# Mixer: the out projection takes y and W_out as single fp32 operands instead of hi and lo halves

## The reference, cut to what matters

```
zxbcdt = x @ W_in                               # 256 -> 512 + 768 + 8
xBC = silu(causal_conv(xBC, 4 taps) + conv_b)   # -> xs, B, C
h = h * exp(dt*A) + dt * x * B ; y = h . C      # scan over tokens, 8 heads of 64, state 128
y = (y + D_skip * xs) * silu(z)
y = y * rsqrt(mean(y*y) + 1e-5) * rms_w
out = y @ W_out                                 # 512 -> 256   <- the product that is changed
y1 = out + x ; g = y1 @ glu_w + glu_b
y2 = y1 + a * sigmoid(gate) ; layer norm ; gate ; add to x
```

## Time and profile before

| | us |
|---|---|
| median of 3 runs | 2222.96 (2219.68, 2222.96, 2231.39) |
| the profiled execution | 2228.17 |
| its span, first to last instruction | 2226.4 |
| PE busy | 1658.3 (74%) |
| DVE busy | 1479.1 (66%) |
| ACT busy | 1053.1 (47%) |
| POOL busy | 1005.1 (45%) |

### The profile page before, as it was taken

One profiled execution on the slowest core, in us unless ns is written; L12 is line 12 of the kernel. 1 busy time (PEld: TensorE's weight loads), 2 busy tenths in 40 slices (PEclk: granted clock), 3 DMA queues, 4 the chain that ended last, 5 costly groups with the idle time before them and its releaser, 6 DMA issues. The chain is left out here.

```text
span 2226.4 us, 37571 instructions
## 1 busy us (share of the span) xinstructions
PE 1658.3 (74%) x10724; PEld 1424.5 (64%) x10725; DVE 1479.1 (66%) x3407; ACT 1053.1 (47%) x2135; POOL 1005.1 (45%) x905
## 2 busy tenths in 40 slices
PE   4757989988999889989887456565319999999300
PEld 4745777777777777777776455454319999999300
DVE  4635788878887788788876566666424444444488
ACT  1315556555655665565564334343206666665200
POOL 1202434443444444334443377777735666666300
PEclk7558999999999999999999666666659999999755
DMA  5421101110111011011010345454334555555599
GB/s 175 153 80 45 35 25 39 39 34 25 39 34 38 26 39 34 24 39 34 29 30 15 115 147 173 145 168 153 131 122 149 177 174 172 176 173 167 211 402 361
DMA packets 148926, 242.12 MB, mean 109 GB/s; under 512 B 24960, under 2 KB 95616, under 8 KB 148608
## 3 DMA queue, kind: packets, MB, share of 16 engines
q1 hardware_dynamic: 122752, 169.77, 24.1%
q0 software_dynamic: 26112, 71.62, 8.8%
HBM read 132.75 MB, written 108.56 MB: 108 GB/s over the span
## 5 line engine op out<-in xcount | busy, mean ns | idle before, releaser
L1997 POOL DMA_INDIRECT ys_dram<-byo,bx x272 | 261.3, 961 | 171.6 <-ACT byo L1930 94.6
L985 DVE SCALAR_TENSOR_TENSOR cv<-xc,convw,cv 128x256 f32<-128x256 f32 x576 | 294.3, 575 | 20.8 <-ACT cv L856 20.8
L1652 POOL DMA_INDIRECT xs_dram<-rows,dest x256 | 264.2, 1032 | 91.9 <-issue 77.1
L1173 POOL TENSOR_TENSOR state<-state,par 128x512 f32<-128x512 f32 x64 | 126.0, 1968 | 283.0 <-PE bank L746 283.0
L1966 DVE TENSOR_TENSOR bff<-bgs,bank 128x256 f32<-128x256 f32 x136 | 57.3, 421 | 212.8 <-ACT bgs L1914 212.8
L1930 ACT ACTIVATE byo<-bank,bx 128x256 f32<-128x256 f32 x272 | 114.3, 472 | 145.3 <-DMA ys_dram<-byo,bx 145.0
L104 PE MATMUL bank<-wh,bhh 128*128 x544 | 160.7, 295 | 8.1 <-ACT bhh L1907 6.0
L106 PE MATMUL bank<-wh,bhl 128*128 x544 | 154.3, 284 | 0.0
L105 PE MATMUL bank<-wl,bhh 128*128 x544 | 153.8, 283 | 0.0
L1184 POOL TENSOR_TENSOR y1l<-y,y1h 128x512 fp32r<-128x512 f32 x32 | 76.2, 2382 | 155.3 <-ACT y1h L912 155.3
L721 PE MATMUL bank<-masked,after 128*128 128x512 f32 x256 | 124.6, 610 | 21.4 <-ACT dec L886 21.4
(11 more groups left out here) (257 smaller groups left out, 5514.0 us busy)
## 6 DMA issues: line engine op xcount, KB each, us to landing
bx<-xs_dram SPq DMA_DIRECT2D x272, 129.0 KB
cy<-ys_dram SPq DMA_DIRECT2D x64, 512.0 KB, 9.2
px<-in_x SPq DMA_DIRECT2D x16, 512.0 KB, 3.6
h_t<-phT SPq DMA_DIRECT2D x16, 512.0 KB, 4.1
hN<-h_t SPq DMA_DIRECT2D x32, 256.0 KB, 2.7
hT<-h_t SPq DMA_DIRECT2D x32, 256.0 KB, 2.6
xr<-in_x SPq DMA_DIRECT2D x32, 256.0 KB, 2.6
x_dram<-xr SPq DMA_DIRECT2D x32, 256.0 KB, 2.0
```

Source lines behind the costliest of these rows:

```text
L985: dve.scalar_tensor_tensor(cv[b][:, m, :], xc[b][:, m, tap:tap + GROUP], convw[:, m, tap:tap + 1], cv[b][:, m, :], ALU.mult, ALU.add).then ...
L1173: pool.tensor_tensor(s, s, par[b][:, 3, c, :].unsqueeze(2).to_broadcast([P, H, HD]), ALU.mult).then_inc(sdec_done[b], 1)
L1652: pool.indirect_dma_start(out=xs_dram[:, :], out_offset=bass.IndirectOffsetOnAxis(ap=dest[n % 2][:, c, k:k + 1], axis=0), in_=rows[n % 2][ ...
L1997: pool.indirect_dma_start(out=ys_dram[:, :], out_offset=bass.IndirectOffsetOnAxis(ap=x[s][:, n, D:D + 1].bitcast(U32), axis=0), in_=yo[s % ...
```

## The change

W_out is kept as one fp32 tile (in place of wout_hi and wout_lo), yT as one fp32 tile (in place of yTh and yTl). ACT still copies both (its outputs are now plain fp32). DVE's subtraction for the W_out piece and its two `split_yT` a half are gone, with their semaphores; whoever waited for yTl waits for yT. `project_out` issues 8 fp32 matmuls of 256 columns in place of 24 fp32r ones. All other pieces keep their order.

```diff
-        pieces.append((t["W_out"], wout[0][:, :, :].rearrange("p a b -> p (a b)"),
-                       wout[1][:, :, :].rearrange("p a b -> p (a b)")))
+        pieces.append((t["W_out"], wout[:, :, :].rearrange("p a b -> p (a b)"), None))
...
+                    if pieces[n][2] is None:
+                        return
                     dve.wait_ge(hi_done, n + 1)
                     dve.tensor_tensor(pieces[n][2], raw[n][:, :], pieces[n][1].bitcast(F32), ALU.subtract)
...
-        wout = [sb(f"wout_{h}", [P, KI, D], F32R) for h in ("hi", "lo")]
+        wout = sb("wout", [P, KI, D])
...
-        yTh = both("yTh", [P, KI, GROUP], F32R)
-        yTl = both("yTl", [P, KI, GROUP], F32R)
+        yT = both("yT", [P, KI, GROUP])
...
                 def project_out(b, i):
-                    pe.wait_ge(yTh_done[b], CH * i + CH)
-                    pe.wait_ge(yTl_done[b], CH * i + CH)
+                    pe.wait_ge(yT_done[b], CH * i + CH)
                     pe.wait_ge(y1s_done[b], CH * i + CH)
                     for m in range(KD):
                         for k in range(KI):
-                            last = split3(pe, Q(b, 2)[:, m * GROUP:(m + 1) * GROUP],
-                                          wout[0][:, k, m * P:(m + 1) * P], wout[1][:, k, m * P:(m + 1) * P],
-                                          yTh[b][:, k, :], yTl[b][:, k, :], k == 0, k == KI - 1)
+                            last = pe.matmul(Q(b, 2)[:, m * GROUP:(m + 1) * GROUP], wout[:, k, m * P:(m + 1) * P],
+                                             yT[b][:, k, :], start=(k == 0), stop=(k == KI - 1))
                     last.then_inc(o_ps[b], 1)
...
-                def split_yT(b, i, c):
+                def take_yT(b, i, c):
                     act.wait_ge(yT_ps[b], CH * i + c + 1)
                     act.wait_ge(o_ps[b], i)
-                    act.activation(yTh[b][:, :, c * P:(c + 1) * P],
+                    act.activation(yT[b][:, :, c * P:(c + 1) * P],
                                    Q(b, c)[:, :].rearrange("p (k t) -> p k t", k=KI),
-                                   ACT.Copy).then_inc(yTh_done[b], 1)
+                                   ACT.Copy).then_inc(yT_done[b], 1)
...
-                def split_yT(b, i, c):
-                    dve.wait_ge(yTh_done[b], CH * i + c + 1)
-                    tok = slice(c * P, (c + 1) * P)
-                    dve.tensor_tensor(yTl[b][:, :, tok], Q(b, c)[:, :].rearrange("p (k t) -> p k t", k=KI),
-                                      yTh[b][:, :, tok].bitcast(F32), ALU.subtract).then_inc(yTl_done[b], 1)
...
                     if second:
                         mean_square(*second, 1)
-                        split_yT(*second, 0)
                     if first:
                         mask_a(*first, 0)
-                    if second:
-                        split_yT(*second, 1)
                     if first:
                         conv(*first, 1)
```

More of the change, by code:

```diff
@@ L568, in mixer @@
         yT_ps = sems("yT_ps", CH)
-        yTh_done = sems("yTh_done", CH)
-        yTl_done = sems("yTl_done", CH)
+        yT_done = sems("yT_done", CH)
         o_ps = sems("o_ps", 1)
@@ L667, in project_xbc @@
                         pe.wait_ge(hTl_done[b], i + 1)
-                        pe.wait_ge(yTl_done[b], CH * i)
+                        pe.wait_ge(yT_done[b], CH * i)
                     if pair == 1:
@@ L953, in half @@
                         squares(*second, 1)
-                        split_yT(*second, 0)
+                        take_yT(*second, 0)
                     if first:
@@ L961, in half @@
                     if second:
-                        split_yT(*second, 1)
+                        take_yT(*second, 1)
                     if first:
```

## The result

| | before | after |
|---|---|---|
| median of 4 runs, us | 2221.32 (2217.75 to 2231.39) | 2279.88 (2277.70 to 2281.52) |
| the profiled execution, its span | 2228.17, 2226.4 | 2277.70, 2275.9 |
| first to last out projection (31 intervals) | 998.1 | 1053.5 |
| start of the first out projection | 214.6 | 211.6 |

The changed kernel is slower: ratio 1.0255, 95% interval 1.022 to 1.0291, +58.6 us between the medians. The forecast was +26 (2249, range 2213 to 2288). The mixer's loop holds the loss: +55.4.

The account below looks back on a forecast made before the run. Bound: a ring of dependences over several engines, with POOL and DVE contending. A half +1.0 - 0.15 + 0.08 = +0.93; 31 halves +28.8, less 3.2, +25.6: median 2223 becomes 2249 us, range 2213 to 2288.

Parts of the forecast that it names:

- Root, +1.0 a half: POOL's root of chunk 1 would stand until DVE's mask_a, moved up beside it, is over: +1.0 us a half.
- yTl(1), -0.15: With chunk 1's yTl subtraction off the path between second transpose and out projection, a half gains about 0.15 us.
- Out projection 3.66: PE's out projection result would be ready about 3.66 us after its start in place of 3.1.
- add_h at 3.66 + 0.1: DVE's add_h would follow PE's out projection, about 0.1 us to wake, 0.08 later than now.
- ratio of 3.44 to 2.94: PE's fp32 out projection against the split one, in us; called close to the 4/3 of 32 passes against 24.
- Whole product: The fp32 out projection's cost to a half: only the 0.08 us by which add_h comes later.
- prepare_tokens, -3.2: Weight stage: DVE no longer waits for ACT's W_out copy nor subtracts, so 3.2 us are gained once.
- Rival A: POOL's root is not held by mask_a; 2218 us, chance 0.20.
- B: POOL's root starves, passed over again by conv of pair 1 and mask_a; 2276 to 2358 us, chance 0.12.
- C: PE becomes the bound and sets add_h later than computed; 2235 us, or 3.4 more a half; chance 0.05.
- Does that delay add_h?: Whether the longer out projection delays DVE's add_h: by 0.08 us a half, glu's wait taking PE's extra 0.5.
- Rival D: Halves with y1l between conv operations disappear, root not held: 2207, chance 0.05; or become common: +25, 2275.

Follow-up runs that it names:

- e1: The changed kernel with DVE's subtraction split_yT for chunk 0 put back, its result unused; ratio 1.0233 to the kernel before, loop 1055.2 us.
- e4: The changed kernel with only mask_a(first, 0) moved behind times_end, where DVE waits for PE; ratio 1.0250 to the kernel before, loop 1055.1 us.
- e2: The changed kernel with both split_yT subtractions put back on DVE, results unused; ratio 1.0094 to the kernel before, loop 1011.4 us.
- e7: The changed kernel with POOL's y1l waiting for the conv of pair 2 and mask_a(first, 0) moved behind times_end; ratio 0.9960 to the kernel before.
- e12: The changed kernel with a useless 128x1536 DVE product added ahead of add_h in each half; ratio 1.0260 to the kernel before, loop 1056.3 us.
- e5b: The changed kernel with POOL made to wait for the conv of pair 2 before y1l; ratio 1.0129 to the kernel before, loop 1026.9 us.

## Why the prediction was wrong

*Root, +1.0 a half: right* for halves at the full clock: 1.46 in place of 0.55, and +0.91 by e1 against after. Taken away alone it gave no time back, in e1 and in e4, because more halves then met the low clock. *yTl(1), -0.15: right.* From the root's end to the out projection it was 2.93, and is 2.70 or 2.86 by turns of the sequence. *Out projection 3.66, add_h at 3.66 + 0.1: right*, 3.62 and 3.65 or 3.75; the records are 0.385 long. (The forecast called its ratio of 3.44 to 2.94 close to 4/3; it is 1.17, and 1.16 was measured.) *Whole product:* 0.13 to 0.21 a half in e2 and e7, where the forecast had nearly nothing. *prepare_tokens, -3.2: right*, by the end of its transposes. Rival A falls by the held root, B because no root was passed over twice, C because in the trace of the changed kernel add_h never came later than 3.77 behind the out projection's start.

*The step that failed* is "Does that delay add_h?". It priced the 0.08 by which add_h comes later and stopped there; that y1l might go early more often stands in the sum at nothing. It did not ask what else changes when DVE has less to do ahead of add_h: y1l became early in 23 more halves. Rival D had this as an afterthought ("if instead they become common ... +25, 2275"), with the right price and no chance of its own, and tied to no edit. By the runs two parts of the change set it off. With the product alone (e2 against before) early halves go from 7 to 17 of 30, 13 of them where PE's product came last; with split_yT(1) gone as well (e1 against e2, which differ in it alone) they go to 30. Why y1l then gets in between the conv operations stays open, as e12 showed. With the early halves come 3 more at the low clock, which no step had.

*The sum in the loop.* A usual half at full clock goes from 31.86 (late) to 33.82 (early, root held): 30 x 1.96 = 58.8. Of this 7 x 1.14 = 8.0 goes off, for the halves that were early before the change. The low clock adds 5 x 1.7 less 2 x 1.57 = 5.4, and the last interval, which has no `first`, is 0.7 shorter. That is 55.5 beside the measured 55.4. Of the 1.96 the root is 0.91 and the early y1l, with the small sizes of the product, yTl(1) and add_h, 1.05. Over the loop the root gives 27, where +1.0 in 31 halves was forecast; the early y1l gives 24 and the low clock 5, where nothing was. With -2.9 ahead of the loop and -3.0 behind it, where no edit is, it is +49.5 between the two spans. The medians are 58.6 apart because the profiled execution of before lay 7 above its median and that of after 2 below.

The measured 2280 lies inside the stated range of 2213 to 2288, and that is luck: the range was drawn so far up for the milder form of rival B, which did not happen. The forecast's own range, 2240 to 2265, missed it.

## What to carry to other kernels

Where operations of two engines hold each other up, as DVE and POOL do here, every place at which both have work is a race, and a change that only gives one of them less to do can turn it in every iteration. Price both outcomes of each such race, with a chance of its own, before summing. Where an operation in between helps no one, let the waiting engine wait for it in so many words: one added wait was worth 26 us here. And before a small operation is taken off an engine, look at what moves up into its place and what runs beside it there.

## What the runs showed of the hardware

- POOL's product of one element a partition, 0.55 alone, takes 1.46 beside a DVE product of two SBUF tiles of 1.21 that started 0.16 before it.
- POOL's y1l beside six successive conv operations of DVE: either 2.7 with the conv at 2.45, or 1.5 with the conv at 4.50. The early form is dearer to the pair though y1l ends sooner: run one after the other, as in e5b, they take 2.46 and 1.27.
- PE goes on after 2.0 us of idleness at a granted clock of 1.00 in some halves and 0.50 in others, with the same instructions; a half pays 1.7 (1.6 in e1). Freeing 0.9 us a half elsewhere raised the number of such halves from 5 to 22 of 30 (e1) and the time stayed.
- An fp32 matmul of 256 columns takes two records of 0.385, which follow one another every 0.215 or so (16 in 3.62), against 3.11 for the 24 fp32r ones of 0.283 each that do the same product in halves.
